# A deeper lookahead in the attention loop, later sums of squares and weight halves, and a new order of the first spline turns

## The reference, cut to what matters

```python
h = relu(layernorm(x))
s, t = (h @ W) @ a[:512], (h @ W) @ a[512:]
e = leaky_relu(s[row] + t[col])                 # one number per edge
att = softmax of e over the edges of each row
agg = segment_sum(att[:, None] * h[col], row)   # 1250 x 512
basis = b_splines(agg)                          # 8 per element, order 3
x = x + silu(agg) @ base_w.T + einsum('nip,oip->no', basis, spline_w)
```

## Time and profile before

| | us |
|---|---|
| median of 3 runs (lowest, highest) | 665.05 (664.79, 665.08) |
| profiled execution | 666.76 |
| its span | 665.0 |
| busy: PE, VectorE, ScalarE, GpSimd | 604.4, 465.5, 369.9, 35.0 |
| share of the chain: PE, VectorE, ScalarE, issue | 74%, 15%, 5%, 3% |

### The profile page before, as it was taken

How to read it: one execution, slowest core, us unless ns; L and a number is a source line. 1 busy time by engine, 2 the same in 40 slices (tenths; PEclk the granted TensorE clock), 3 DMA queues, 4 the chain that set the end, 5 groups by cost and what they waited for, 6 DMA issues and landing times.

```text
span 665.0 us, 9149 instructions
## 1 busy us (share of the span) xinstructions
PE 604.4 (91%) x3641; PEld 432.4 (65%) x3641; DVE 465.5 (70%) x731; ACT 369.9 (56%) x487; POOL 35.0 (5%) x40
## 2 busy tenths in 40 slices
PE   3766797889998999999999999699999999999994
PEld 2545674446564555555555555378999899988994
DVE  7989997899767999996389755973345335452354
ACT  1797886766789998984498413149213313132121
POOL 2000510000000000000000001102200020000000
PEclk9897767989998999999999999989999999999997
DMA  8554400000040000000001000460200000002102
GB/s 288 193 191 129 200 1 0 2 0 2 0 156 0 2 1 0 1 1 1 0 1 64 1 0 1 169 247 0 64 1 1 0 1 1 0 0 83 71 39 116
DMA packets 11418, 33.75 MB, mean 51 GB/s; under 512 B 718, under 2 KB 1038, under 8 KB 11120
## 3 DMA queue, kind: packets, MB, share of 16 engines
q1 hardware_dynamic: 11376, 33.17, 14.0%
HBM read 24.78 MB, written 8.40 MB: 50 GB/s over the span
## 4 chain that ended last, share of the span: by engine, by line
PE 74%; DVE 15%; ACT 5%; issue 3%; DVEq 1%; ACTq 0%; DMA 0%; SPq 0%
PE bank L1511 32%; PE bank L1586 21%; PE bank L1555 12%; PE bank L1436 7%; DVE OM L867 3%; DVE OR L864 3%; DVE JH L942 2%; ACT JSQ L562 1%; DVE MSK L961 1%; DVE SCR L969 1%; DVE AL L1009 1%; PE bank L1447 1%; ACT CT L630 1%; PE bank L1453 1%; DVE XL L1232 1%
## 5 line engine op out<-in xcount | busy, mean ns | idle before, releaser
L1511 PE MATMUL bank<-BHL,WKh 128*128 128x418 f16 x1152 | 206.2, 340 | 2.1 <-DVE BHL L1097 2.1
L1511 PEld LDWEIGHTS bank<-BHL,WKh 128*128 128x128 f16 x1152 | 111.7, 97 | 96.6 <-issue 2.6
L1586 PE MATMUL bank<-CF,YL 128*128 128x418 f32 x360 | 127.5, 354 | 0.0
L1586 PE MATMUL bank<-CF,YH 128*128 128x418 f32 x360 | 126.6, 352 | 0.0
L1287 DVE TENSOR_TENSOR Z<-bank,dvb 128x418 f32<-128x418 f32 x36 | 21.3, 592 | 69.1 <-PE bank L1586 69.1
L1586 PEld LDWEIGHTS bank<-CF,YL 128*128 128x128 f32 x360 | 67.6, 188 | 1.8
L1586 PEld LDWEIGHTS bank<-CF,YH 128*128 128x128 f32 x360 | 67.6, 188 | 1.0
L801 ACT ACTIVATE bnc<-bnm,tiny 128x1 f32<-128x1 f32 x12 | 3.5, 295 | 105.2 <-DVE bnm L1293 105.2
L1345 PE MATMUL bank<-OM,OR 128*128 128x160 f16 x320 | 32.2, 267 | 19.7 <-DVE OM L867 14.7
L1238 DVE SCALAR_TENSOR_TENSOR YL<-bank,dvc,YH 128x512 fp32r<-128x512 f32 x30 | 21.9, 748 | 38.5 <-ACT YH L782 38.5
L1555 PE MATMUL bank<-GWH,XH 128*128 128x512 f32 x120 | 48.5, 404 | 0.0
(11 more groups left out here) (203 smaller groups left out, 1029.2 us busy)
## 6 DMA issues: line engine op xcount, KB each, us to landing
WKf<-in_wk SPq DMA_DIRECT2D x9, 1024.0 KB, 5.4
c_scratch<-C SPq DMA_DIRECT2D x1, 3200.0 KB, 11.0
GWf<-in_gwT SPq DMA_DIRECT2D x3, 1024.0 KB, 5.2
C<-c_scratch SPq DMA_DIRECT2D x1, 2880.0 KB, 10.6
XT<-in_xT SPq DMA_DIRECT2D x1, 2500.0 KB, 8.7
x_scratch<-XT SPq DMA_DIRECT2D x1, 2500.0 KB, 16.3
XR<-x_scratch SPq DMA_DIRECT2D x1, 2500.0 KB, 9.1
outT<-Z SPq DMA_DIRECT2D x4, 625.0 KB, 3.1
```

Of the source, the lines that this page charges most:

```text
L1511: ins = mm(bank[:, 4 * (g % 2) + o, 0:G], lhs, rhs, start=(u == 0 and q == 0 and i == 0), stop=(u == UNITS - 1 and q == PAIR - 1 and i == 2))
L1586: ins = mm(bank[:, YB + u % YB, 0:G], Y[:, j, o * P:(o + 1) * P], CF[:, j, g * G:(g + 1) * G], start=(j == 0 and i == 0), stop=(j == NT - ...
```

## The change

EX gets a fourth buffer and moves to another place (where slots 4 and 5 of BHL lie, which the turns write after the loop). Sums and exponentials run two steps ahead, and VectorE's order within a step becomes low part of n-2, sum of n+2, product of n. ScalarE's last four sums of squares move from steps 1, 3, 5, 7 to 4, 7, 10, 13; VectorE's adding from step 9 to 15, TensorE's matmul from group 0 to group 1 behind tile 5 (bank 5 for bank 2), the scale from step 13 to 19; the ten high halves from steps 16 to 25 to 20 to 29, the low halves with them. In the turns, `middle(1)` and `nearest(1)` go behind the squares of turn 0, and the cast of turn 0 goes ahead of the squares of turn 1.

```diff
+EXS = 4
-LATE_SQUARES = (1, 3, 5, 7)
+LATE_SQUARES = (4, 7, 10, 13)
-FIRST_HALF = 16
+FIRST_HALF = 20
-        EX = at("EX", Z1 + 11424, [3, G], F32)
+        EX = at("EX", Z1 + 9752, [EXS, G], F32)
...
             exponentials(0)
+            exponentials(1)
             for n in range(NG * NT):
                 g, j = divmod(n, NT)
-                if n + 1 < NG * NT:
-                    exponentials(n + 1)
+                if n + 2 < NG * NT:
+                    exponentials(n + 2)
...
             clipped(0)
-            middle(1)
-            nearest(1)
             for n in range(NG * TURNS):
...
+                if n == 1:
+                    turn_high(0)
                 squares_of(n, i)
+                if n == 0:
+                    middle(1)
+                    nearest(1)
...
-                elif n >= 1:
+                elif n >= 2:
                     turn_high(n - 1)
...
-                if n >= 3:
-                    dve.wait_ge(att_low, n - 2)
+                if n >= EXS:
+                    dve.wait_ge(att_low, n - EXS + 1)
...
-                V.tensor_scalar(wsc[:, 1:2], bank[:, 2, 0:1], 1e-30, None, ALU.add)
+                V.tensor_scalar(wsc[:, 1:2], bank[:, 5, 0:1], 1e-30, None, ALU.add)
...
             attention_sum(0)
+            attention_sum(1)
             for n in range(NG * NT):
-                if n + 1 < NG * NT:
-                    attention_sum(n + 1)
-                if n >= 1:
-                    attention_low(n - 1)
+                if n >= 2:
+                    attention_low(n - 2)
+                if n + 2 < NG * NT:
+                    attention_sum(n + 2)
                 attention_f32(n)
-                if n == 9:
+                if n == 15:
                     dve.wait_ge(squares, KB)
                     V.tensor_reduce(wsc[:, 0:1], wss[:, :], AX, ALU.add).then_inc(sumsq_set, 1)
-                if n == 13:
+                if n == 19:
                     weight_scale()
...
+            attention_low(NG * NT - 2)
             attention_low(NG * NT - 1)
...
                 if g == 1:
                     pe.wait_ge(pq_set, NG)
+                if g == 2:
                     pe.wait_ge(wscale_set, 1)
...
                         attend(g, k, j)
+                    if g == 1 and j == 5:
+                        pe.wait_ge(sumsq_set, 1)
+                        pe.wait_ge(agg_out, DC)
+                        mm(bank[:, 5, 0:1], ones[:, :], wsc[:, 0:1], start=True, stop=True).then_inc(sumsq_done, 1)
...
-                    if g == 0 and k == 1:
-                        pe.wait_ge(sumsq_set, 1)
-                        pe.wait_ge(pq_set, NG)
-                        mm(bank[:, 2, 0:1], ones[:, :], wsc[:, 0:1], start=True, stop=True).then_inc(sumsq_done, 1)
```

More of the change, by code:

```diff
@@ L613, in exponentials @@
                 act.wait_ge(att_sum, n + 1)
-                nc.scalar.activation(EX[:, n % 3, :], EX[:, n % 3, :], ACT.Exp, bias=mx[:, 5, n % NT:n % NT + 1]
+                nc.scalar.activation(EX[:, n % EXS, :], EX[:, n % EXS, :], ACT.Exp, bias=mx[:, 5, n % NT:n % NT + 1]
                                      ).then_inc(exps, 1)
@@ L624, in _ @@
             exponentials(0)
+            exponentials(1)
             for n in range(NG * NT):
                 g, j = divmod(n, NT)
-                if n + 1 < NG * NT:
-                    exponentials(n + 1)
+                if n + 2 < NG * NT:
+                    exponentials(n + 2)
                 act.wait_ge(att_f32, n + 1)
-                nc.scalar.copy(CT[:, j, g * G:(g + 1) * G], EX[:, n % 3, :]).then_inc(att_high, 1)
+                nc.scalar.copy(CT[:, j, g * G:(g + 1) * G], EX[:, n % EXS, :]).then_inc(att_high, 1)
                 if n == 0:
@@ L998, in attention_sum @@
                 dve.wait_ge(pq_set, g + 1)
-                if n >= 3:
-                    dve.wait_ge(att_low, n - 2)
+                if n >= EXS:
+                    dve.wait_ge(att_low, n - EXS + 1)
                 cols = slice(g * G, (g + 1) * G)
-                V.scalar_tensor_tensor(EX[:, n % 3, :], PQ[:, 0, cols], mx[:, 4, j:j + 1], PQ[:, 1, cols], ALU.add, ALU.max
+                V.scalar_tensor_tensor(EX[:, n % EXS, :], PQ[:, 0, cols], mx[:, 4, j:j + 1], PQ[:, 1, cols], ALU.add, ALU.max
                                        ).then_inc(att_sum, 1)
@@ L1008, in attention_low @@
                 cols = slice(g * G, (g + 1) * G)
-                V.tensor_tensor(low_weights(g)[:, j, :], EX[:, n % 3, :], CT[:, j, cols], ALU.subtract).then_inc(att_low, 1)
+                V.tensor_tensor(low_weights(g)[:, j, :], EX[:, n % EXS, :], CT[:, j, cols], ALU.subtract).then_inc(att_low, 1)
             def attention_f32(n):
@@ L1013, in attention_f32 @@
                 dve.wait_ge(exps, n + 1)
-                V.scalar_tensor_tensor(EX[:, n % 3, :], EX[:, n % 3, :], 2.0, CT[:, j, g * G:(g + 1) * G], ALU.min, ALU.mult
+                V.scalar_tensor_tensor(EX[:, n % EXS, :], EX[:, n % EXS, :], 2.0, CT[:, j, g * G:(g + 1) * G], ALU.min, ALU.mult
                                        ).then_inc(att_f32, 1)
```

## The result

The changed kernel takes 663.69 us (median of 21 runs, 662.84 to 665.67) against 665.10 (664.15 to 668.4) of the kernel before; the ratio is 0.9972, 95% interval 0.9961 to 0.9983, so 1.1 to 2.6 us faster. A second set gives 0.9959 (0.9942 to 0.9975). Forecast was 659.4 with 662.2 as the upper end: right in direction, but 5.7 us where 1.4 were measured, four times too much.

The account below looks back on a forecast made before the run. TensorE was taken as nearly the whole bound from 188.27 us on, leaving the attention handover and spline start to win. Loop 3.1 + turns 1.0 + clock 1.6 = 5.7 us off the 665.05 median gave 659.4 us, range 658.2 to 662.2.

Parts of the forecast that it names:

- The clock: Gap before the spline units: shortened from 2.1 to 1.2 us, it keeps the granted clock high; 1.6 us won.
- Loop: Attention: two steps of lookahead and later squares end it at 185.2 instead of 188.27 us, 3.1 us won.
- (a): Gap before the spline units: the shorter gap also drops the clock; 4.1 us won, 661.0 us; chance 0.25.
- self-wait of the sum: VectorE's attention step: the sum waiting for the low part just ahead costs 0.12 us, bounds 0 and 0.28.
- a constant 1.1 us: Group 0 of attention: 1.1 us added for TensorE's first matmuls at the low clock, as now.
- VectorE starts at 102.93 as before: Start of the attention loop: VectorE begins at 102.93 us, unchanged.
- Turns: Start of the spline units: new order of casts and squares starts TensorE 18.14 us after attention, not 19.1; 1.0 us won.
- The scale's wait: Step 19 of attention: VectorE waits 4.4 us for the sum-of-squares matmul where it waited for nothing.
- nothing is late: Behind the first turns: TensorE waits nowhere in L1511, so the whole lead reaches the end.
- (b): Attention: ScalarE does not make up for the squares, or waits reach their upper bound; 1.9 us won, 663.1 us; chance 0.07.
- (c): Attention from step 20: ScalarE a step late, eight weight low parts wait up to 1.14 us each; 670.0 us; chance 0.03.
- (d): Attention and turns: the wait for the scale takes all the gain, the turn order gains nothing; 665.0 us; chance 0.03.

Follow-up runs that it names:

- only the loop: Changed kernel with the new order of the first two turns taken back; 665.83 us, ratio 0.9990 against the kernel before.
- only the turns: Kernel before with only the new order of the first two turns; 664.44 us, ratio 0.9976.
- 10: Changed kernel with 12 and 3 filler matmuls ahead of attention, 70 and 40 at the last LayerNorm group; 662.09 us, ratio 0.9943.
- 12: Changed kernel with filler matmuls ahead of attention, before the first spline unit (25) and at the last LayerNorm group; 662.74 us, ratio 0.9951.
- warm start alone: Kernel before with 12 and 3 filler matmuls ahead of attention, results unused; 664.16 us, ratio 0.9971.

## Why the prediction was wrong

**Two terms of the sum failed:** the 1.6 us of the clock, together with the last line that took the whole 5.7 off the median, and the 3.1 us of the loop.

**The clock, forecast 1.6.** The forecast read 1.6 us of low clock in the one profile, booked them as won, and carried them over to the median. But that execution took 666.76 us where the median was 665.05; the repeat of the same kernel took 664.57, with the same gap, and had no low clock there. Of the four profiles with the old turn order and no filler in that gap, two have K at 223.05 and two at 221.42. What the change removes is a chance of this loss, not the loss: 0.8 us on average by these profiles, and less at the median, which lies in the lower group of executions. The forecast drew from the Trainium skill (TensorE: Matmul & The Clock Gate, "What's actually happening") that equal gaps can come out either way, since the instant of a change of clock is not tied to the kernel; the pairs of profiles bear it out. It had been set against the *changed* kernel as rival (a); it should have been set against the base.

**Loop, forecast 3.1, measured 1.2 on average, 0.5 to 1.4 with a warm start.** Three parts of the miss are inside attention. (1) The base: B of 85.34 was at the upper end of 83.75 to 85.35, again by the clock (0.6 ahead of the scale, A of 29.35 against 28.73, where TensorE's last spreads before attention ran low; and 0.9 at the first spread). (2) The self-wait of the sum, forecast at 0.12 a step with 0.28 as its bound, costs 0.18: 0.4 at the reciprocals of group 0 (A 42.5, forecast 42.1) and 0.5 behind the scale (B less A is 40.7, forecast 40.2). (3) A new exposure, which the forecast had as a constant 1.1 us: in the changed order a TensorE that starts low runs without a wait from its first attention matmul to the matmul that the scale waits for, and one that starts high waits 1.0 us at the first spread, so only about that much of a low clock at the start is covered. A is 42.5 when it starts at 1.00, 43.2 to 43.8 when it starts at 0.50; in the old order VectorE set that pace and the same start cost nothing.

**"VectorE starts at 102.93 as before", a term at nothing.** In nine of twelve profiles of the new loop it starts later, 0.6 us on average over all twelve. If that is the change's, the loop is left with 0.6 of its 1.2 us, which is what "only the loop" measured (ratio 0.9990, that is 0.7 us, its interval including nothing). It isn't shown that it is the change's.

As an estimate from the averages of the profiles: 1.2 (loop) + 0.9 (turns) + 0.8 (clock behind the gap) - 0.6 (later start) - 0.7 (N at 34.6 in three of seven, below) = 1.6 us, against 1.4 and 2.7 between the medians of the two sets.

**Turns, forecast 1.0:** right, 0.9 in each profile (19.10 to 18.18).

**The scale's wait, forecast 4.4:** 3.8 and 4.3. Right, and it is the costliest part of the change: it is why earlier low parts in group 0 bring so little.

**Behind the turns, "nothing is late":** right for the order (K and N are the same to 0.05 us where the clock is), but not for the clock. In three of the eleven profiles without fillers at the LayerNorm and with its old place N is 34.6, never in the five with fillers. All three have the new order of the turns. The executions without a profile fit: of the changed kernel 12 of 21 took up to 663.93 us and nine 664.35 or more, of "only the turns" eight of 12 up to 664.44 and four 665.26 or more, while with fillers at the LayerNorm (10 and 12) all 12 lie within 1.1 us. Whether the new order's earlier arrival makes this loss likelier, or the profiles fell so, is not settled: three of seven profiles of the new order against none of four of the old don't tell.

**The rivals.** (a) was wrong as put: the clock fell behind the 1.2 us gap in none of eleven profiles. (b) gave 663.1, near the result, but for other reasons: ScalarE did make up for the squares (VectorE never waits for a cast in group 0) and the self-wait stayed under its bound, so its nearness is luck. (c) did not occur. Of (d) the time of "only the loop" has something, but not the reason: the scale's wait was no longer than forecast.

Left open: why the warm start alone made the kernel before 0.3% faster. Its one profile is of one of its longer executions, and none of the 12 is in the upper group of the kernel before; how the fillers ahead of attention would keep the clock up in a gap 100 us later is not shown.

## What to carry to other kernels

Compare the profiled execution with the median before pricing a loss in it; a loss that the median lacks can't be won in full. A clock drop is a chance attached to a gap, so take two or three profiles of the base before booking one, and compare variants by several profiles each: two programs that were the same up to the end of attention differed there by 0.9 us. And when a queue is made faster, look for the engine that inherits the pace: its start at the low clock and the next cross-engine wait (the scale, then the reciprocals) become the price.

## What was not expected of the hardware

An operation on VectorE that waits for the one just ahead of it starts 0.69 us after it instead of 0.51 (operations of 418 columns, 0.59 us long): 0.10 behind its end, not the 0.04 seen behind small ones. Matmuls whose result nobody reads, put into waits of 1 to 6 us, kept the granted clock at 1.00 in those places, and with the ones at the last LayerNorm group the spread of the changed kernel fell from 2.8 us (21 runs) to 0.7 and 1.0 us (6 runs each); those ahead of attention alone left it at 3.1 (12 runs).
